# A macaron block with two routed FFNs: slots that carry token and share, a scatter into the output, and a reordered last gate and start

## What is computed

```python
x = x + 0.5 * ffn(layernorm(x))          # top-1 of 8 experts, 2048 tokens of 128, hidden 512
x = x + attn(layernorm(x))               # the gated recurrence over 4 sequences of 512
x = x + 0.5 * ffn(layernorm(x))          # the same experts again

def ffn(x):
    probs = softmax(x @ w_router)        # the routing weight is the largest one
    for e in range(8):
        y = relu(x @ w1[e] + b1[e]) @ w2[e] + b2[e]
        out += (chosen == e) * weight * y

def attn(x):                             # 8 heads of 64
    xn = layernorm(x);  x_t, r_t = xn @ W_up_l.T, xn @ W_up_r.T
    x_c = silu(conv4(x_t));  q, k, gates, skip from x_c;  v, o from x_t
    h = sigmoid(o) * recurrence(q, k, v, gates)
    return ((layernorm_per_head(h) * mh_g + mh_b + skip) * silu(r_t)) @ W_down.T + b_down + x
```

## Time and profile before

| what | us |
|---|---|
| median of the runs | 464.28 |
| lowest and highest of 3 | 463.85, 469.93 |
| the profiled execution | 463.59 |
| its span, first to last instruction | 461.8 |
| PE busy | 408.3 (88%) |
| DVE busy | 343.4 (74%) |
| ACT busy | 219.8 (48%) |
| POOL busy | 125.7 (27%) |

### The profile page before, as it was taken

The page is one execution under the profiler, slowest core; times in us unless marked ns, Lnnn a source line. Parts: engine busy times, 40 slices in busy tenths (PEclk is TensorE's granted clock), DMA queues, the critical chain, the costliest instruction groups (busy, mean ns, idle before and its releaser), DMA issues.

```text
span 461.8 us, 10342 instructions
## 1 busy us (share of the span) xinstructions
PE 408.3 (88%) x3127; PEld 331.2 (72%) x3150; DVE 343.4 (74%) x1048; ACT 219.8 (48%) x567; POOL 125.7 (27%) x125
## 2 busy tenths in 40 slices
PE   5439899998999999999999999999999999979970
PEld 5413899934877788877778777788768965769970
DVE  3685577667449989779989689989699785747763
ACT  2641444424465565545584654555555721624430
POOL 5276244520003101121111021111031067534450
PEclk9999999999999999999999999999999869989995
DMA  9991222169900000000000000000001301212216
GB/s 284 375 399 58 59 71 68 57 202 362 361 30 0 3 1 1 1 0 0 0 0 0 0 0 0 0 0 0 1 1 25 160 24 40 59 51 64 68 52 182
DMA packets 25662, 35.35 MB, mean 77 GB/s; under 512 B 3521, under 2 KB 17729, under 8 KB 25121
## 3 DMA queue, kind: packets, MB, share of 16 engines
q1 hardware_dynamic: 21554, 26.24, 17.4%
q0 software_dynamic: 2496, 5.13, 3.3%
q10 hardware_dynamic: 1584, 3.63, 2.3%
HBM read 17.52 MB, written 17.47 MB: 76 GB/s over the span
## 4 chain that ended last, share of the span: by engine, by line
issue 39%; PE 32%; POOL 10%; DVE 8%; DMA 6%; ACT 3%; SPq 1%; DVEq 0%; POOLq 0%; ACTq 0%
PE bank L865 28%; POOL HS L537 4%; POOL slots L497 4%; DMA QKT<-by_token 2%; DMA XB<-slots 2%; DMA slots<-XN,POS 1%; PE bank L886 1%; ACT WVT L755 1%; PE bank L994 1%; DMA by_token<-YB,IDX 1%; ACT E L764 1%; DMA WR<-w_router 1%; POOL LA L531 1%; PE bank L1215 1%; DVE X L1365 1%
## 5 line engine op out<-in xcount | busy, mean ns | idle before, releaser
L537 POOL TENSOR_TENSOR HS<-HS,MHALF 128x8 f32<-128x8 f32 x16 | 26.4, 1647 | 150.7 <-DVE HS L1931 150.7
L521 POOL DMA_INDIRECT by_token<-YB,IDX x46 | 44.1, 959 | 52.7 <-DVE YB L1621 51.5
L755 ACT ACTIVATE WVT<-bank,AC 128x128 f32<-128x128 f32 x128 | 36.7, 377 | 37.4 <-PE bank L865 37.4
L865 PE MATMUL bank<-XBT,W1R 128*128 128x128 f32 x368 | 50.2, 280 | 0.3 <-ACT XBT L657 0.3
L865 PE MATMUL bank<-W,HT 128*128 x368 | 49.5, 278 | 0.0
L865 PEld LDWEIGHTS bank<-XBT,W1R 128*128 128x128 f32 x368 | 45.5, 195 | 0.9 <-ACT XBT L657 0.5
L865 PEld LDWEIGHTS bank<-W,HT 128*128 128x128 f32 x368 | 45.5, 194 | 0.4
L865 PE MATMUL bank<-MASKB,IDB 128*128 128x512 bf16 x157 | 40.8, 392 | 1.6 <-DMA QKT<-by_token 0.5
L497 POOL DMA_INDIRECT slots<-XN,POS x32 | 32.7, 1022 | 21.3 <-issue 15.6
L1615 DVE TENSOR_SCALAR HT<-bank,W1R 128x128 f32<-128x128 f32 x92 | 28.0, 346 | 12.9 <-PE bank L865 11.2
L719 ACT ACTIVATE QKT<-bank,COLS 128x512 f32<-128x512 f32 x32 | 22.0, 688 | 32.5 <-PE bank L865 32.5
(11 more groups left out here) (339 smaller groups left out, 975.8 us busy)
## 6 DMA issues: line engine op xcount, KB each, us to landing
slots<-FILL SPq DMA_DIRECT2D x37, 258.0 KB, 5.6
W<-w SPq DMA_DIRECT2D x2, 2048.0 KB, 15.1
XB<-slots SPq DMA_DIRECT2D x46, 64.5 KB, 1.9
W<-w SPq DMA_DIRECT2D x1, 2064.0 KB, 15.7
QKT<-by_token SPq DMA_DIRECT2D x8, 256.0 KB, 4.0
slots<-QKT SPq DMA_DIRECT2D x1, 1483.5 KB, 11.4
X<-x SPq DMA_DIRECT2D x4, 256.0 KB, 5.7
out<-X SPq DMA_DIRECT2D x4, 256.0 KB, 2.5
```

What stands on the lines that cost most here:

```text
L521: g.indirect_dma_start(out=by_token[f], out_offset=bass.IndirectOffsetOnAxis(ap=IDX[:, j:j + 1], axis=0), in_=YB[:, j, :], in_offset=None) ...
L537: g.tensor_tensor(HS[:, 3, :], HS[:, 2, :], MHALF[:, 0:H], ALU.pow).then_inc(roots_ready, 1)
L755: ins = a.activation(DT[:, hf, m, :], DM[:, m * P:(m + 1) * P], ACT.Exp, bias=AC[:, c, h:h + 1])
L865: return t_.matmul(o, l, r, start=start, stop=stop, skip_group_check=True)
```

## The change

The second FFN's slots are 258 wide instead of 129: the normalised row, the token number, the row of X itself and the share. The share is half the routing weight. To have it early, the exponentials and `shares` are split into 12 early and 4 late tiles. SyncE copies the early rows of X into the wide rows (`XN1`), and the last two tiles of X are written there directly. In a turn of the second FFN the bias buffer becomes bias x share + x, and the result y x share is added to it, so the scatter writes rows of the final output straight to `out`; a bounds check drops unused slots. The read-back, the combine and the store of the second FFN go. ScalarE takes three relu chunks there and VectorE one. The last chunk's gate multiplies skip term and `mhg` ahead of the root, `squares` goes before the copy of the transposed output, the list of experts is made before the list of rows, and the fillers are fewer. At the start five weight loads move from ScalarE's queue to behind the fill on SyncE's, which now waits for all of x; 11 filler matmuls on a tile of ones stand first. In the first head, `reset_state` and `silu` come before the last combine, and `add_u` after the gate scans.

```diff
@@ slots and tiles
+SHARE = SLOT + D
+SLOT1 = SHARE + 1
...
-    slots = [nc.dram_tensor(f"slots_{f}", [n * P, SLOT], F32, kind="Internal").ap()
-             for f, n in enumerate((NBLK, NFILL * FROWS))]
+    slots = [nc.dram_tensor(f"slots_{f}", [n * P, w], F32, kind="Internal").ap()
+             for f, (n, w) in enumerate(((NBLK, SLOT), (NFILL * FROWS, SLOT1)))]
...
+        def x_at(f, t):
+            return XN1[:, t, SLOT:SHARE] if f == 1 and t >= NT - 2 else X[:, t, :]
@@ SyncE
             sp.wait_ge(fill_made, 1)
+            sp.wait_ge(x_loaded[3], 16)
             sp.dma_start(slots[0].rearrange("(p k) w -> p k w", p=P), FILL).then_inc(slots_filled[0], 16)
+            for dst, src in ((WULT[:, :], wult), (WURT[:, :], wurt), (WVT[:, :, :], wvt), (WOT[:, :, :], wot),
+                             (WIFT[:, :, :], wift)):
+                sp.dma_start(dst, src).then_inc(folds_loaded, 16)
...
-                        sp.dma_start(rows.rearrange("(p k) w -> p k w", p=P), FILL1[:, :, :]).then_inc(slots_filled[1], 16)
+                        rows = rows.rearrange("(p k) w -> p k w", p=P)
+                        for at in (0, SLOT):
+                            sp.dma_start(rows[:, :, at:at + SLOT], FILL1[:, :, :]).then_inc(slots_filled[1], 16)
                     sp.wait_ge(*pj_full_at(NB - 1, "s3"))
+                    sp.wait_ge(*tr_read_at(NB - 2, "d3"))
+                    sp.dma_start(XN1[:, 0:EARLY, SLOT:SHARE], X[:, 0:EARLY, :]).then_inc(x_copied[0], 16)
                     sp.dma_start(W2[:, :, :, :], w2).then_inc(w2_loaded, 16)
+                    sp.wait_ge(*tr_read_at(NB - 1, "d1"))
+                    sp.dma_start(XN1[:, EARLY:NT - 2, SLOT:SHARE], X[:, EARLY:NT - 2, :]).then_inc(x_copied[1], 16)
...
-            for g in range(4):
-                sp.wait_ge(ffn_done[1], 4 * g + 4)
-                sp.dma_start(out_v[:, 4 * g:4 * g + 4, :], X[:, 4 * g:4 * g + 4, :]).then_inc(out_stored, 16)
-            sp.wait_ge(out_stored, 64)
@@ POOL
+                        ins = g.indirect_dma_start(out=out, out_offset=number, in_=YB[:, j, :], in_offset=None,
+                                                   bounds_check=NT * P - 1, oob_is_err=False)
...
-                pool.wait_ge(slots_filled[1], 16 * NFILL)
+                pool.wait_ge(slots_filled[1], 32 * NFILL)
+                pool.wait_ge(x_copied[0], 16)
                 pool.wait_ge(pos_ready[1], 1)
+                pool.wait_ge(share_ready, 1)
@@ ScalarE
+                    if f == 1 and t == NT - 2:
+                        exponentials(1, EARLY, NT)
...
-                    for c in range(2):
+                    for c in range(2 + f):
...
+                if last:
+                    squares(b, 3)
+                    out_t(b, 2)
@@ TensorE
+                    pe.wait_ge(ones_made, 1)
+                    for _ in range(11):
+                        mm(bank[7][:, :], MASKB[:, 0:P], MASKB[:, :])
...
-                    spin(17)
+                    spin(9)
                     transpose_out(b, 2)
                     spin(3)
                     down_out(b, 2)
-                    spin(22)
+                    spin(14)
                     pe.wait_ge(roots_ready, NB * NC)
-                    spin(14)
+                    spin(6)
...
             pe.wait_ge(tanh_ready, 1)
-            spin(5)
+            spin(7)
@@ VectorE, in a turn
+                        v.tensor_copy(PB[:, j:j + 1], XB1[:, j, SHARE:SLOT1])
+                        dve.wait_ge(w1_copied[f], k + 1)
+                        v.scalar_tensor_tensor(out=B2R[:, j, :], in0=B2R[:, j, :], scalar=XB1[:, j, SHARE:SLOT1],
+                                               in1=XB1[:, j, SLOT:SHARE], op0=ALU.mult, op1=ALU.add)\
                             .then_inc(idx_copied[f], 1)
...
+                        ins = v.scalar_tensor_tensor(out=YB[:, j, :], in0=bank[6 + j % 2][:, 0:D], scalar=PB[:, j:j + 1],
+                                                     in1=B2R[:, j, :], op0=ALU.mult, op1=ALU.add)
@@ VectorE, first head
+                combine(1)
+                combine(2)
+                reset_state()
+                silu(0)
+                combine(3)
+                low_xc(0)
@@ VectorE, last chunk
+            def last_addend(b):
+                did(v.tensor_tensor(SK[3], SK[3], GR[3], ALU.mult))
+            def last_gate_scale():
+                did(v.tensor_tensor(GR[3], GR[3], row("mhg", HID), ALU.mult))
+            def last_scale():
+                did(v.tensor_tensor(flat, flat, GR[3], ALU.mult))
+            def last_products(b):
+                dve.wait_ge(roots_ready, NC * b + 4)
+                do(v.tensor_tensor(H2[:, :, :], H2[:, :, :], bc(HS[:, 3, :], [P, H, HD]), ALU.mult))
+                v.tensor_tensor(OUT[:, :], flat, SK[3], ALU.add).then_inc(outg_ready, 1)
...
                 if last and c == 3:
+                    last_addend(b)
                     weigh(b, 3, 1)
+                    last_gate_scale()
                     scale_q(b, 3)
                     early_choice()
```

198 lines of the change are left out of this document (115 added, 83 removed).

## The result

| | before | after |
|---|---|---|
| median of four runs | 464.06 us | 450.19 us |
| profiled execution | 463.59 us | 452.01 us |
| its span | 461.8 us | 450.2 us |

The ratio is 0.972, with a 95% interval of 0.966 to 0.979. The forecast was 447.5 us, a ratio of 0.964. Of the four runs, the profiled one is the slowest. So the change made the kernel faster, by about 2.5% where 3.6% was forecast.

What follows compares the result with a forecast made beforehand. No engine is busy throughout; chains of waits bound the kernel. Tail 10.6, start 3.0, first head 3.0, last chunk 0.9, less turns 1.0, make 16.5 us: 463.59 becomes 447.1, stated as 447.5 for the median; range 443.5 to 453.

Steps and rivals of the forecast that it cites:

- Tail: Kernel's end: removing read-back, combine, store and late shares closes the span at 451.2, gaining 10.6 us (8.4 to 11.1).
- Rival (e): Kernel's end: the checked scatter is slow, 5 us remain and the time is 453 us; chance 0.04.
- Start: Before the first scatter: wide matmuls raise TensorE's clock and x arrives sooner, gaining 3.0 us.
- the lower of my cases: Start: narrow matmuls bring the clock down again halfway, choice of an expert at 13.8, gain 2.2 us.
- first needed near 29: Start: weights moved behind the fill arrive later, but their wait lies beside 20 us of scatters.
- First head: First attention head: XC sooner, gates at 111.5 without a gap, no half level after; gain 3.0 us (1.4 to 3.2).
- The second half: First attention head: without the gap, no half level in the following 3.4 us, which returns 1.7 us.
- Fill: Filling the second FFN's wider slots: 53 us by bytes or 211 by pieces, 275 us available, cost 0.
- rival (d): Second slots' fill not done when early scatters want it, deciding from 116 ns a piece; slower kernel, chance 0.03.
- Last chunk: Last attention chunk: transposes at 387.4 instead of 389.04, 1.5 us; gain 0.9 by the fifth block (1.5 to -0.7).
- Turns: Second FFN's 18 turns: added VectorE work and slot reload cost 0.5 us each, 1.0 in all.
- Rival (a): Second FFN: VectorE bounds the turn, costing 4 to 5 us instead of 1.0, time 451 us; chance 0.17.

Runs made afterwards that it cites:

- the second trace of the changed kernel: The changed kernel, unaltered, run again beside later kernels on another chip; ratio 0.978 (0.974 to 0.982) to the kernel before.
- the experiment: Changed kernel with the first head's old order and 5 instead of 7 fillers ahead of the gates; ratio 0.978 (0.973 to 0.983) to the kernel before.
- the second trace of the kernel before: Kernel before with only its closing changed, GpSimd not drained before the closing barrier; ratio 1.001 (0.998 to 1.003) to the kernel before.

## Why the prediction was right or wrong

**Tail: the mechanism right, the size wrong.** The term was 10.6 us with bounds of 8.4 and 11.1. It measured 5.7 (11.6 less the 5.9 at the last scatter). The step that failed is "the SyncE waits and the closing steps that remain I put at 0.5 us". The steps of SyncE are that short, but GpSimd's drain is a closing step as well. It had its row in the trace of before, 7.8 us from 448.07 on, and wasn't asked for, since the chain of waits shows only 0.30 us of it, ahead of the last scatter. Only what the end waited for shows there, so whoever takes away the end of a chain has to ask what was running beside it. Rival (e), the checked scatter slow, gave 453 us for a loss of this size; it has the right size and the wrong mechanism: the check costs 0.5 us ahead of the scatter and nothing in flight.

**Start: 3.2 us at the first scatter, forecast 3.0**, with the choice at 12.8 between my 11.4 and 13.8. In this trace the clock holds through all narrow matmuls and falls only behind them. The eleven solid matmuls raised it: behind them 8 logit matmuls take 1.06 and 0.96 us, where they take 1.87 and 1.71 without the warm-up. The 4.6 us worked out for a clock that holds were not reached here: the eleven ran at the half level to their end at 6.30, the first eight transposes took 1.55 us, and TensorE's last logits ended at 12.74, with VectorE free at 12.09; the forecast had VectorE as the limit, at 11.4. Of the ten traces with the warm-up and x alone, eight have the choice between 11.76 and 12.78 and the first scatter 3.2 to 4.2 us sooner than before. In two the choice stood at 14.34 with the 16 matmuls at 3.42 us, near the lower of my cases, and the gain is 1.7 us. So 3.0 was a middle between two outcomes rather than a value that the kernel takes. The GHz beside the two levels in the forecast are estimates. What the trace of the kernel before shows is the pace of the fillers of 512 columns: 0.427 us from one to the next at a granted clock of 0.50 (seven weight loads from 374.40 to 376.96), and 0.213 us at 1.00 (four fillers in 1.02 us at 394.34; a single one takes 0.38). That is 1.2 and 2.4 columns a nanosecond; that a column takes one clock, which makes GHz of it, is the author's assumption and no run shows it.

What the forecast missed is what becomes of it: of the 3.2 us only 1.5 were left at the first FFN's last sum. The step was that the weights are "first needed near 29" and that the wait "lies beside 20 us of scatters". Most of it does, yet VectorE stood 5.55 us until 39.41, the folds ended only 0.5 us before the rows, and the first transposes came 2.5 us sooner instead of 3.2. That copy of the weights stands between 37.6 and 40.5 in all fourteen traces, with the old order of the transfers as with the new, so an earlier start is in part spent on waiting for it; in the second trace of the changed kernel the chain of waits passes through it. Another 1.0 us went at sum 5, which stood behind late rows of block 8. It did so in five of the ten traces with the new start (2.6 to 2.9 us between two sums) and not in the five others (1.8 us); why is open.

**First head: forecast 3.0, in the traces 3.3, by the experiment 1.0 to 1.7.** The first half (1.4 us for the gap) is right. The second half (1.7 us returned by the clock) credited the edit with a stretch at the half level that the kernel before has in one of its two traces and not in the other. A right number for half a reason.

**Fill: cost 0, right.** It ran from 96 to about 222, 126 us, with almost 150 us to spare before the first early scatter. That lies about midway between the bounds of 53 and 211, at 53 ns a piece and DMA engine, far below the 116 from which rival (d) would have decided.

**Last chunk: forecast 1.5 at the transposes, measured -0.7.** The first early scatter came 0.75 us later relative to the rest, just as said, and the output was there 1.5 us sooner. The step that failed is the choice between two named cases: "if the 2.7 us that TensorE is now idle bring the half level, it is 388.9: nothing". It did in this trace, and the fillers, counted for the full level, ran 4.0 us past the output. Block 5 came 4.3 us sooner instead of 6.9. The other case, the full level, is in two traces: the transposes stand 23.7 us behind the early logits, 2.2 us sooner than in the trace of the kernel before from which the forecast was worked out. But the second trace of the kernel before has 23.1 itself, so the two executions of one kernel differ here by more than the whole term, and what the edit is worth stays open.

**Turns: forecast -1.0, measured 0 or better.** From sum 7 to sum 19 it is 22.85 us after and 23.17 before, 1.90 and 1.93 a turn. Rival (a) is wrong. From block 5 to the last sum 2.3 us came back that no term had: before, this stretch had 3.4 us at the half level behind an idle of 3.43 us, and 2.40 us between sums 6 and 7; after, there is no half level behind the shorter idle of 2.14 us. It is the same kind of luck as at the head, since the second trace of the changed kernel does have the half level there, from 405.8, behind an idle of only 1.35 us.

**The sum.** Ahead of the tail I had 5.9 us and the trace has 5.9, but by compensation: 1.5 us less than forecast by the first FFN's last sum and 1.4 less over the last chunk, against 0.3 more at the head and 2.7 more from block 5 to the last scatter (2.3 us gained there, and 0.6 us lost again ahead of the last scatter, where 1.0 was to be lost). What is left is the tail's 4.9 us: the sum gave 447.1 for the profiled execution, 447.1 and 4.9 make 452.0, and it took 452.0. The median, 450.19, lies 2.7 us above the 447.5 forecast for it. That the time came out near the forecast but for the tail owes as much to errors that cancel as to the terms.

## What to carry to other kernels

Before the end of a chain is cut, look at every closing instruction of every engine, GpSimd's drain above all: here it ended 6.45 us behind the last indirect transfer in all three traces that were read for it, and it cost nothing (1.001) only in the kernel whose other work ran for 13.35 us beside and behind it; without such work it was 5.0 us.

The warm-up here was worth what the work behind it finished before TensorE stood idle again: with all of x there the choice came at 12.78, with the last quarter of x 1.96 us late at 16.14, and without the warm-up at 16.43. So the data's arrival and the clock have to be planned as one edit. And a stretch at the half level in one trace is not a property of the kernel (behind the first head the two traces of the kernel before print 0.58 and 1.00): compare two traces before it is put on an edit's account, and look for a wait that is filled at the next wait in line, as here, where the 2.8 us ahead of the down product went and 2.69 us came at the late choice.

## What the runs showed of the hardware

- GpSimd's closing drain ended 6.45 to 6.46 us behind the end of its last indirect scatter in the first trace of the kernel before and in both of the changed kernel; in the eight traces of the changed kernel and its variants with the drain the span ended 6.6 to 6.7 us behind that end. Without the drain it ended 2.7 us behind the start of the scatter.
- The bounds check on an indirect scatter delayed its start by 0.5 us (from 0.28 to 0.78 us behind the data), added 0.02 us to its 0.96 us on GpSimd, and left its flight as it was (2.2 us from start to landing).
- After eleven 512-wide matmuls (4.3 to 4.9 us) TensorE ran 32 narrow matmuls (8 in 1.06, 8 in 0.96, 16 in 1.91 us) and the transposes between them (4 in 0.64 us) at the full level in eight of ten traces; in the changed kernel's first trace the next matmuls, after 1.68 us without work, took 0.42 us each where one of that shape takes 0.27 later, and the granted clock is 0.53 there (14 to 18): the half level. In the other two traces it fell before the last 16 of them.
- The half level in one place comes and goes between executions: around a stand of 2.4 to 3.5 us in the last chunk it came in six of eight traces with the same fillers, and not in two, where the stand was 3.0 us.
- The profile prints a granted clock of 1.00 for the first 40 us of the kernel before, while 16 matmuls take 3.42 us there and the same 16 take 1.90 us at 363.07: in this stretch the durations tell the level, the printed clock does not.
- Two executions of one kernel part by up to 3.3 us at a sum for which VectorE waits though its data is there; the cause is open.
